# A feed-forward hand-over on one core: which engine rounds the modulated tokens, and in which order

## The reference

```python
c6 = silu(c) @ Wc + bc
sh_msa, sc_msa, g_msa, sh_mlp, sc_mlp, g_mlp = split(c6, 6, axis=-1)
xm = ln(x) * (1 + sc_msa) + sh_msa
q, k, v = xm @ Wq + bq, xm @ Wk + bk, xm @ Wv + bv      # 16 heads of 32
w = softmax(einsum("bqhc,bkhc->bhqk", q / DH, k))
y = einsum("bhqk,bkhc->bqhc", w, v)
x = x + g_msa * (y @ Wo + bo)
xm2 = ln(x) * (1 + sc_mlp) + sh_mlp
h = gelu(xm2 @ W1 + b1)
x = x + g_mlp * (h @ W2 + b2)
```

## Time and profile before

| | us |
|---|---|
| median of 3 runs | 2948.07 (2947.85 to 2952.06) |
| the profiled execution, its own time | 2950.05 |
| its span | 2948.2 |
| TensorE busy | 2863.9 (97%) |
| VectorE busy | 2033.7 (69%) |
| ScalarE busy | 1339.6 (45%) |
| GpSimd busy | 1998.3 (68%) |

### The profile page before, as it was taken

One profiled execution on the slowest core, in us unless ns is written; L12 is line 12 of the kernel. 1 busy time (PEld: TensorE's weight loads), 2 busy tenths in 40 slices (PEclk: granted clock), 3 DMA queues, 4 the chain that ended last, 5 costly groups with the idle time before them and its releaser, 6 DMA issues. The chain is left out here.

```text
span 2948.2 us, 40747 instructions
## 1 busy us (share of the span) xinstructions
PE 2863.9 (97%) x14713; PEld 1815.9 (62%) x14713; DVE 2033.7 (69%) x3384; ACT 1339.6 (45%) x2535; POOL 1998.3 (68%) x1012
## 2 busy tenths in 40 slices
PE   7999999999999999999999999998699999999998
PEld 5777555555555555555555555552587777777777
DVE  5444587777777777777777777773757757766764
ACT  2222156666666666666666666665111111111111
POOL 1000079999999999999999999996554545545453
PEclk9999789999999999999999999999799999999999
DMA  6444832422414314323324324202201101100000
GB/s 229 171 172 164 212 69 57 97 66 66 110 43 99 90 34 106 79 61 90 72 65 97 81 52 98 69 24 97 104 1 44 43 1 44 43 21 23 29 15 15
DMA packets 152766, 225.19 MB, mean 76 GB/s; under 512 B 31804, under 2 KB 48760, under 8 KB 152568
## 3 DMA queue, kind: packets, MB, share of 16 engines
q1 hardware_dynamic: 123036, 204.81, 25.6%
q10 hardware_dynamic: 29532, 17.79, 2.1%
HBM read 162.30 MB, written 58.97 MB: 75 GB/s over the span
## 5 line engine op out<-in xcount | busy, mean ns | idle before, releaser
L839 DVE TENSOR_REDUCE part_max<-m_bank 128x1 f32<-128x512 f32 x2048 | 1252.1, 679 | 395.0 <-PE m_bank L925 394.9
L820 ACT ACTIVATE probs<-s_bank 128x512 f32<-128x512 f32 x2048 | 1035.3, 626 | 241.7 <-PE s_bank L939 237.6
L939 PE MATMUL s_bank<-qs,ks 97*128 97x512 f32 x2048 | 847.0, 415 | 2.5 <-ACT probs L820 2.2
L722 POOL TENSOR_TENSOR low_sum<-probs 128x1024 f32<-128x1024 f32 x248 | 589.2, 2387 | 121.4 <-ACT probs L820 121.2
L737 POOL TENSOR_TENSOR high_sum<-high_sum,probs 128x1024 f32<-128x1024 f32 x256 | 608.4, 2376 | 42.5 <-ACT probs L820 5.7
L939 PEld LDWEIGHTS s_bank<-qs,ks 97*128 97x128 f32 x2048 | 385.9, 189 | 342.1 <-issue 211.2
L949 PE MATMUL y_bank<-probs,vs 128*32 128x512 f32 x4096 | 497.3, 603 | 0.0
L1315 ACT ACTIVATE h<-up_bank,vecs 128x512 f32<-128x512 f32 x128 | 88.2, 689 | 634.9 <-PE up_bank L1340 634.9
L730 POOL TENSOR_TENSOR high_sum<-probs 128x1024 f32<-128x1024 f32 x128 | 308.0, 2406 | 13.0 <-ACT probs L820 13.0
L949 PEld LDWEIGHTS y_bank<-probs,vs 128*32 128x32 f32 x4096 | 107.5, 109 | 243.7 <-issue 133.6
L1139 POOL TENSOR_TENSOR w_lo<-space_plain,w_hi 128x512 fp32r<-128x512 f32 x64 | 87.3, 1365 | 206.1 <-DVE w_hi L1224 206.1
(11 more groups left out here) (141 smaller groups left out, 3797.4 us busy)
## 6 DMA issues: line engine op xcount, KB each, us to landing
qs<-q_parts SPq DMA_DIRECT2D x96, 256.0 KB, 5.6
ks<-k_parts SPq DMA_DIRECT2D x96, 256.0 KB, 5.1
q_parts<-qk_out SPq DMA_DIRECT2D x32, 512.0 KB, 3.4
k_parts<-qk_out SPq DMA_DIRECT2D x32, 512.0 KB, 3.4
xb<-in_x SPq DMA_DIRECT2D x12, 1024.0 KB, 7.5
space_parts<-q_parts SPq DMA_DIRECT2D x48, 256.0 KB, 4.9
space_parts<-k_parts SPq DMA_DIRECT2D x48, 256.0 KB, 4.6
late_parts<-k_parts SPq DMA_DIRECT2D x48, 256.0 KB, 4.5
```

The source lines that it names most:

```text
L722: pool.tensor_tensor(low_sum[:, (2 * c + half) % 4, :, :], probs[:, first % RING, hs, :], probs[:, (first + 1) % RING, hs, :], ALU.add).th ...
L820: act.activation(probs[:, tile % RING, h, :], s_bank[(HPG * tile + h) % 3][:, :], ACT.Exp).then_inc(p_done, 1)
L839: v.tensor_reduce(part_max[:, i % 2, hs, c:c + 1], m_bank[ring.bank["max", i, n]][:, :], AX.X, ALU.max).then_inc(m_taken, 1)
L939: pe.matmul(s_bank[n % 3][:, :], ks[:, h, t * P:(t + 1) * P], qs[i % 2][:, h, :], start=True, stop=True).then_inc(s_done, 1)
```

## The change

In the feed-forward:

- The rounding of the modulated tokens, `xm` to `xm_hi`, goes from VectorE to ScalarE, as an activation with Copy. A new function `round_xm` does the four pieces behind the last `gelu` of a block (and behind the four modulations at the start), and has the wait for `up_done`. VectorE's `split_xm` keeps the four subtractions.
- At j = 15 VectorE does `split_h` alone. The two weight roundings that it did there (for `up` of step 1 and `down` of step 0 of the next block) follow behind the four subtractions.
- The output projection's tiles go to `o_bank` and `t_bank` in turn, and a tile waits for the eviction of the one before the last, not of the last.

```diff
+        wo_bank = [o_bank, t_bank]
...
-            def residual(k, q, b, t, bank=o_bank):
+            def residual(k, q, b, t, bank=None):
 
                 n = TT * k + t
+                if bank is None:
+                    bank = wo_bank[t % 2]
                 v.wait_ge(wo_done, 1 + n + 1)
...
             def split_xm(k):
-                v.wait_ge(up_done, MT * k + 2)
                 for t in range(KT):
-                    v.wait_ge(t_taken, 1 + KT * k + t + 1)
-                    v.tensor_copy(xm_hi[:, t, :], xm[:, t, :]).then_inc(xm_hi_step, 1)
                     v.wait_ge(xm_hi_step, KT * k + t + 1)
                     v.tensor_tensor(xm_lo[:, t, :], xm[:, t, :], xm_hi[:, t, :].bitcast(F32), ALU.subtract).then_inc(xm_split, 1)
...
                 for j in range(1, MT):
-                    parts_for(k, j, has_next or j < MT - 2, has_next or j < MT - 1)
+                    if has_next and j == MT - 1:
+                        split_h(MT * k + j, j)
+                    else:
+                        parts_for(k, j, has_next or j < MT - 2, has_next or j < MT - 1)
...
                 if has_next:
                     split_xm(k + 1)
+                    high_w1(MT * (k + 1) + 1, 1)
+                    high_w2(MT * (k + 1), 0)
                 result_gated(k, b)
...
+            def round_xm(k):
+                act.wait_ge(up_done, MT * k + 2)
+                for t in range(KT):
+                    act.wait_ge(t_taken, 1 + KT * k + t + 1)
+                    act.activation(xm_hi[:, t, :], xm[:, t, :], ACT.Copy).then_inc(xm_hi_step, 1)
...
+                if has_next:
+                    round_xm(k + 1)
 
             bias_y(0)
             for t in range(KT):
                 modulate(0, 0, t, first_t[t])
+            round_xm(0)
...
                 if bank is None:
-                    bank = o_bank
-                    pe.wait_ge(wo_taken, TT * k + t + 1)
+                    bank = wo_bank[t % 2]
+                    pe.wait_ge(wo_taken, TT * k + t)
```

## The result

| | before | after |
|---|---|---|
| median | 2948.98 us (2947.85 to 2952.06, 6 runs) | 2932.05 us (2929.17 to 2934.25, 6 runs) |
| ratio | | 0.9941, 95% interval 0.9928 to 0.9953 |
| the profiled execution, own time | 2950.05 | 2929.17 |
| its span | 2948.2 | 2927.4 |

The kernel became 16.9 us faster between the medians; the interval of the ratio puts the gain between 13.9 and 21.2 us. The forecast was 2931.0, with 17.1 us. Of these, 15.9 lie in the seven hand-overs and 2.8 in the first block. The other 2.2 us lie ahead of the feed-forward's first transposes (the last matmul of the first projections starts at 2088.31, against 2090.49), in code that the change does not touch. So positions are compared here within the feed-forward only.

A forecast was written before the change was run, and what follows sets the result against it. TensorE was taken as the bound, held at hand-overs by VectorE's chain. 16.1 us at seven hand-overs plus 1.0 in the first block made 17.1 us, so a median of 2931.0 us, range 2926 to 2938.

The forecast's parts named there:

- What bounds the kernel: TensorE, busy 97% of the span; its feed-forward hand-over waits follow VectorE's chain, at most 24.8 us to win.
- The three waits: TensorE's waits at block hand-overs for xm_lo (7 times), h_lo (7) and y_lo (6), claimed to be one lateness.
- The sum at the hand-over: result starts 2.30 us earlier at each of the seven hand-overs between blocks, 16.1 us in all.
- The place of the gain: VectorE's chain at the hand-over: four roundings, a wait and blocked parts of three instructions go; result 2.30 us earlier.
- the 0.66 us wait: VectorE's wait ahead of the w2 rounding at the hand-over, claimed to go away with the change.
- the blocked instructions: VectorE instructions held beside GpSimd, 1.67 instead of 0.69 us; rival: one more per hand-over 2938 us (12%), one fewer 2925 (6%).
- ScalarE's rounding: Four xm roundings behind the block's last gelu, pace 0.61 us, 0.71 for one; last ends at 2315.24.
- The turning point: Rival of slow ScalarE rounding at hand-overs: decides at d = 1.77 us per rounding; at 2.0, 2955 us median; 3%.
- The weight roundings: Two weight roundings behind the xm subtractions, first 2.4 us later; delay covered with 1.9 us to spare.
- The banks: Two banks for the output projection: claimed to gain nothing, as TensorE never waits for wo_taken.
- The first block: Start of the feed-forward: 1.1 to 1.5 us won, part lost to the clock; 1.0 taken, ends -3 and +1.5.
- Rivals: One more blocked instruction 12%, one fewer 6%, table load 3%, stall stays 5%, slower through ScalarE's rounding 3%.

The follow-up runs named there:

- A: Against the kernel before: only the rounding of xm moved to ScalarE, weight roundings and single projection bank left as they were; 2936.93 us, ratio 0.9951.
- B: Against the kernel before: only the order changed, VectorE still rounds xm but the two weight roundings stand behind the four pieces; 2935.50 us, ratio 0.9945.
- both F: Changed kernel with each ScalarE rounding of xm done twice (2933.46 us, ratio 0.9937) or three times (2954.15 us, ratio 1.0002), except in the first block.
- E: Against the kernel before: ScalarE rounds xm in the first block alone, VectorE in all later blocks; 2949.17 us, ratio 0.9991.
- C: Against the kernel before: only the two banks for the output projection; 2951.59 us, ratio 0.9998.
- K: Against H: in the first block ScalarE rounds each piece of xm right behind its modulation; 2918.78 us, ratio 0.9881 to before.
- H: Against the changed kernel: ScalarE rounds y too, VectorE keeps the y subtractions; 2919.33 us, ratio 0.9888 to before.

## Why the prediction was right

*What bounds the kernel.* Right. The three waits were one lateness, and the end of VectorE's chain set it. Over six kernels (before, after, A, B and both F) the period is 103.85 plus the lag above 5.70. Three of them (after, B and the twofold rounding) lie at 5.70 or 5.71; of the others, A has a lag of 6.25, which gives 104.40 (measured 104.4); before has 7.97, which gives 106.12 (106.1); the threefold rounding 8.35, which gives 106.50 (106.5).

*The sum at the hand-over.* 2.30 us forecast, 2.27 at `result` and 2.27 in the mean period measured. Seven of them are 15.9 us. That the medians differ by 16.9 where 17.1 was forecast is closer than the measurement can tell, and partly luck: hand-overs and first block add up to 18.7 in the profile.

*The place of the gain.* The number was right, but the prediction's text counted the four roundings, the 0.66 us wait and the blocked instructions as one removal. The runs show that they overlap: the order alone gives 2.27, the move alone 1.72, both together 2.27. The floor of 5.70 is set by TensorE's first `up` product and `gelu` behind it, and either way VectorE's chain is short enough to reach it.

*ScalarE's rounding.* The bounds were 0.599 to 0.71 for one at a pace of 0.61. Four take 2.18 us, so the pace is 0.52 and one takes 0.62, within them. After 2100 us the trace shows one table load, of 1.28 us, as before. The Trainium skill ("ScalarE: Activation LUTs", "Table sets: the hidden batching unit") says that copy lies in every set; the trace agrees for the table of Gelu, with 32 roundings by Copy and no load for them.

*The turning point.* It was put at d = 1.77 us. With d = 1.85 the period is 0.37 above that of before, where 4 x (1.85 - 1.77) gives 0.3. That there is slack below was right too: 1.19 costs nothing. Where between 1.19 and 1.85 the cost begins was not measured.

*The weight roundings.* In the changed kernel GpSimd's first subtraction starts at 2309.50 and ends at 2310.90, 2.1 us before TensorE wants it; forecast 1.9.

*The banks.* Nothing, as forecast.

*The first block.* The term that was mis-sized: 1.0 us forecast with ends of -3 and +1.5, 2.8 in the profile of the changed kernel, and 1.6 to 3.5 between the profiles of the kernels with ScalarE's rounding of `xm` there (after, A, E, both F) and those without (before, B, C). The shorter chain was sized rightly, at the lower end of its 1.1 to 1.5: TensorE starts the last of the four pieces 17.9 us behind the projections instead of 19.0, 1.1 us earlier. What was wrong was to let the clock take some of that back; it gave another 1.7 us in the changed kernel, and 0.6 in A and E. The clock came back earlier in all profiles with ScalarE's rounding. By the durations of the matmuls it was back 16 to 21 us behind the projections there (11 in K), and 23 to 25 us in those with VectorE's rounding. That the denser product is the cause is argued, not shown.

*Rivals.* None happened. The blocked instructions behind `result` kept their places (`result` 4.69 us both times, `y_lo` wait 4.7 us in total both times).

## What to carry to other kernels

When several waits of the bound engine follow each other and the engine behind them shows no idle time in between, they are one chain; price a change by how much earlier the chain's last link starts, and look for the floor that the bound engine itself sets to it. Test the parts alone: here moving two short instructions behind a more urgent group did in the steady state all that the whole change did, and more than the move to another engine alone. The next gain lay in the same chain, in the same kind of instruction, on an engine with free time.

## What the runs showed of the hardware that was not expected

The granted clock in the first block was back between 11 and 25 us after the last projection matmul, over all kernels here. Five of them (after, A, E, both F) do the same work up to the end of the first `up` product, and TensorE starts each of its four pieces at the same distance from the projections, within 0.02 us. Still the clock was back after 16.2 us in one and 20.6 in another, and the block's length moved with it from 117.8 to 119.0 us. A difference of one or two microseconds there can't be read from one profile.

VectorE's subtractions last longer beside GpSimd, as its roundings do (1.67 instead of 0.69 us, and 1.5 instead of 0.42), so taking the roundings away does not end the blocking: in H both `y` subtractions of a pair were held.
